# A two-layer block on one core: the step-size chain is moved mostly to GpSimd, C's rows are moved by DMA, and all four engines get a new order in the state-space stage

## What is computed

```python
zxbcdt = u @ W_in.T                    # z 512, x 512, B 64, C 64, dt 4
xBC = silu(conv4(xBC))                 # causal, 4 taps per channel
dt  = softplus(dt + dt_bias)           # per token and head: the step size
A   = -exp(A_log) * dt                 # per token and head: the decay rate
# chunks of 128 tokens:
Y_diag = ((C @ B.T) * exp(segsum(A))) @ (x * dt)
states = decayed previous state + (B * decay).T @ (x * dt)
Y_off  = (C @ previous state) * exp(cumsum(A))
y = (Y_diag + Y_off + D * x) * silu(z); y = rmsnorm(y) @ W_out.T
x3 = layernorm(x2 + y)
```

## Time and profile before

| | us |
|---|---|
| median of 3 runs | 1286.04 (1283.23 to 1286.77) |
| profiled execution, its time | 1287.44 |
| profiled execution, its span | 1285.2 |
| PE busy | 1212.8 |
| state-space steps | from 652 to 989 |

### The profile page before, as it was taken

How to read it: one execution, slowest core, us unless ns; L and a number is a source line. 1 busy time by engine, 2 the same in 40 slices (tenths; PEclk the granted TensorE clock), 3 DMA queues, 4 the chain that set the end, 5 groups by cost and what they waited for, 6 DMA issues and landing times.

```text
span 1285.2 us, 20958 instructions
## 1 busy us (share of the span) xinstructions
PE 1212.8 (94%) x7192; PEld 1033.5 (80%) x7192; DVE 853.5 (66%) x1590; ACT 612.3 (48%) x1240; POOL 444.8 (35%) x577
## 2 busy tenths in 40 slices
PE   6899999999999999999989999999998899999994
PEld 5777888888888888888867777777776788888884
DVE  4787635444353535443668988889853889999995
ACT  3443323232333323233467878888874444444441
POOL 0345200000000000000068878878773334444343
PEclk8999999999999999999989999999998899999998
DMA  5222101001010101000000101111010101111100
GB/s 181 83 82 86 34 1 30 5 1 34 1 34 1 33 0 43 6 1 17 13 30 25 39 10 45 45 45 37 8 46 25 34 1 33 33 33 33 33 17 33
DMA packets 30393, 41.29 MB, mean 32 GB/s; under 512 B 2432, under 2 KB 22912, under 8 KB 30208
## 3 DMA queue, kind: packets, MB, share of 16 engines
q1 hardware_dynamic: 30336, 40.53, 9.7%
HBM read 27.94 MB, written 12.58 MB: 32 GB/s over the span
## 4 chain that ended last, share of the span: by engine, by line
PE 75%; DVE 15%; issue 4%; ACT 3%; POOL 2%; DMA 1%; DVEq 0%; POOLq 0%; ACTq 0%; SPq 0%; PEldq 0%
PE bank L45 23%; PE bank L47 22%; PE bank L46 22%; DVE acc L1260 3%; PE bank L1854 1%; DVE mag L1090 1%; PE bank L1835 1%; DVE acc L1256 1%; ACT hh L719 1%; PE bank L1759 1%; DVE dden L1281 1%; DVE wf L1098 1%; PE bank L1594 1%; PE bank L1816 1%; DVE hb L1166 1%
## 5 line engine op out<-in xcount | busy, mean ns | idle before, releaser
L1166 DVE TENSOR_TENSOR hb<-gl,bank 128x512 f32<-128x512 f32 x128 | 87.9, 687 | 198.9 <-PE bank L47 196.3
L719 ACT ACTIVATE hh<-hb 128x512 fp32r<-128x512 f32 x128 | 80.9, 632 | 182.9 <-DVE hb L1166 182.9
L758 ACT ACTIVATE gl<-bank 128x512 f32<-128x512 f32 x128 | 76.4, 597 | 180.7 <-PE bank L47 180.5
L1129 DVE TENSOR_TENSOR hl<-hb,hh 128x512 fp32r<-128x512 f32 x128 | 96.3, 752 | 84.5 <-ACT hh L719 84.5
L702 POOL TENSOR_TENSOR dhl<-dab,dhh 128x512 fp32r<-128x512 f32 x64 | 96.5, 1529 | 141.8 <-ACT dhh L719 141.8
L547 POOL TENSOR_TENSOR veb<-mvb,eps 128x4 f32<-128x4 f32 x8 | 1.8, 228 | 377.7 <-DVE mvb L1146 377.7
L45 PE MATMUL bank<-xt_l,w_h 128*128 128x512 f32 x256 | 105.4, 412 | 8.8 <-DVE xt_l L1129 4.5
L47 PE MATMUL bank<-xt_h,w_h 128*128 128x512 f32 x256 | 103.2, 403 | 0.0
L45 PE MATMUL bank<-at_l,w_hi_a 128*128 128x512 f32 x256 | 102.5, 400 | 0.5 <-PE bank L47 0.3
L46 PE MATMUL bank<-xt_h,w_l 128*128 128x512 f32 x256 | 103.0, 402 | 0.0
L47 PE MATMUL bank<-at_h,w_hi_a 128*128 128x512 f32 x256 | 101.7, 397 | 0.0
(11 more groups left out here) (234 smaller groups left out, 3642.7 us busy)
## 6 DMA issues: line engine op xcount, KB each, us to landing
xg<-x_scratch SPq DMA_DIRECT2D x16, 512.0 KB, 4.0
xall<-in_x SPq DMA_DIRECT2D x8, 512.0 KB, 7.6
xg<-in_xt SPq DMA_DIRECT2D x8, 512.0 KB, 5.0
x_scratch<-rows_out SPq DMA_DIRECT2D x8, 512.0 KB, 3.2
x_scratch<-rows_out SPq DMA_DIRECT2D x16, 256.0 KB, 2.2
out<-rows_out SPq DMA_DIRECT2D x8, 512.0 KB, 3.1
wq<-in_codes SPq DMA_DIRECT2D x12, 256.0 KB, 2.7
sc<-in_scales SPq DMA_DIRECT2D x12, 256.0 KB, 2.9
```

What stands on the lines that cost most here:

```text
L719: return act.activation(dst, src, ACT.Copy)
L758: act.activation(gl[:, n % 2], ps_gate[n % 2][:], ACT.Gelu_apprx_tanh).then_inc(s_gelu, 1)
L1129: return dve.tensor_tensor(dst, src, hi.bitcast(F32), ALU.subtract)
L1166: dve.tensor_tensor(hb[:, n % 2], gl[:, n % 2], ps_up[n % 2][:], ALU.mult).then_inc(s_h, 1)
```

## The change

- `dt_ratio` and `dt_and_rate` go from DVE to POOL. DVE keeps four instructions: the bias, -|d|, u, and one reciprocal (`dt_inverse`). The guard on u - 1 and the one on the logarithm are replaced by one maximum in the instruction that makes u. POOL gets seven small `tensor_tensor` for a group, max(d, 0) made as a subtraction and a multiplication. One more in all negates the decay rate ahead of the first.
- `c_rows` (C's 64 partitions copied to partitions 0 to 63, `ct`) goes from a DVE copy to a DMA on SP's queue, except for the first group.
- `inv_std_chunk` for each chunk becomes `inv_std_pair` for two chunks.
- The lanes of PSUM are dealt anew, and with them the waits; all four `step` functions have another order. SP loads the weight piece after the rows instead of ahead of them, since `mlp1_low` stands later on POOL.

```diff
-DT_STEPS = 11
+DT_STEPS = 4
+DTP_STEPS = 7
+TINY = 2.0 ** -23
...
-        T_LANE = (lane_q, lane_p)
-        DT_LANE = lane_p
-        XBC_LANE = (lane_q, lane_r, lane_q, lane_r, lane_r)
-        def acs_lane(n):
-            return lane_q if isinstance(n, int) and n == 0 else lane_p
+        T_LANE = (lane_p, lane_q)
+        XBC_LANE = (lane_p, lane_r, lane_p, lane_r, lane_q)
+        ACS_LANE = lane_q
+        def dt_lane(n):
+            return lane_p if isinstance(n, int) and n == 0 else lane_r
         def z_lane(n, t):
             if isinstance(n, int) and n == 0:
                 return (lane_p, lane_r, lane_r, lane_p)[t]
-            return (lane_p, lane_p, lane_p, lane_q)[t]
+            return (lane_q, lane_q, lane_p, lane_q)[t]
         def seg_lane(t, more=True):
-            return (lane_r, lane_p, lane_r if more else lane_q, lane_p if more else lane_q)[t]
+            return (lane_r, lane_r, lane_r, lane_p)[t] if more or t == 0 else lane_q
...
+            def c_rows(n, b):
+                sp.wait_ge(c_silu, XB * n + 1)
+                sp.dma_start(ct[:, b], bc[D_STATE:2 * D_STATE, b]).then_inc(c_ct, 16)
...
             def step(s, b, i, more):
                 k = NT * s
                 if more or b == 0:
-                    sp.wait_ge(c_w1l, s + 1)
-                    sp.dma_start(w1_raw[:], w_mlp1[s + 1]).then_inc(c_w1r, 16)
+                    c_rows(s + 1, 1 - b)
                 if more:
                     sp.wait_ge(c_rest, s + 1)
                     sp.dma_start(xg[:, b], x2_rows[b * GPB + i + 1]).then_inc(c_xg[b], 16)
@@ -485,6 +494,9 @@
                         sp.wait_ge(c_x3st[half], 16 * s + 16)
                     sp.wait_ge(c_rest, s + 1)
                     sp.dma_start(xg[:, 0], x3_rows[0]).then_inc(d_x, 16)
+                if more or b == 0:
+                    sp.wait_ge(c_w1l, s + 1)
+                    sp.dma_start(w1_raw[:], w_mlp1[s + 1]).then_inc(c_w1r, 16)
                 store_x3(b, i, 0, k)
...
+            def dt_ratio(n):
+                pool.wait_ge(c_dtc, DT_STEPS * n + 3)
+                pool.tensor_tensor(um[:], du[:], ones[:, 0:NT * HEADS], ALU.subtract).then_inc(c_dtq, 1)
+                pool.tensor_tensor(dtwo[:], dax[:], d_flat, ALU.subtract).then_inc(c_dtq, 1)
+                pool.wait_ge(c_dtq, DTP_STEPS * n + 2)
+                pool.tensor_tensor(dpos[:], dtwo[:], m_half[:, 0:1].broadcast_to([P, NT * HEADS]), ALU.mult).then_inc(c_dtq, 1)
+            def dt_and_rate(n, b):
+                pool.wait_ge(c_dtc, DT_STEPS * (n + 1))
+                pool.tensor_tensor(dq[:], de[:], drec[:], ALU.mult).then_inc(c_dtq, 1)
+                pool.wait_ge(c_dta, 2 * n + 2)
+                pool.wait_ge(c_dtq, DTP_STEPS * n + 4)
+                pool.tensor_tensor(dm2[:], dq[:], dl[:], ALU.mult).then_inc(c_dtq, 1)
+                pool.wait_ge(c_dtq, DTP_STEPS * n + 5)
+                pool.tensor_tensor(dtv[:, b].rearrange("p t h -> p (t h)"), dpos[:], dm2[:], ALU.add).then_inc(c_dtq, 1)
+                pool.wait_ge(c_dtq, DTP_STEPS * n + 6)
+                if not isinstance(n, int) or n > 0:
+                    pool.wait_ge(c_acs, n)
+                pool.tensor_tensor(adt[:], dtv[:, b], na4[:].unsqueeze(1).broadcast_to([P, NT, HEADS]),
+                                   ALU.mult).then_inc(c_dtq, 1)
             def rates_split(n):
-                pool.wait_ge(c_dtc, DT_STEPS * (n + 1))
+                pool.wait_ge(c_dtq, DTP_STEPS * (n + 1))
...
+            def inv_std_pair(k, c):
+                two = slice(c, c + 2)
+                pool.wait_ge(c_ln3, 2 * k + 4)
+                pool.tensor_tensor(ve[:, two], mv[:, two, 1], eps4[:, 0:2], ALU.add).then_inc(c_ln3r, 1)
+                pool.wait_ge(c_ln3r, 2 * k + 1)
+                pool.tensor_tensor(rstd[:, two], ve[:, two], m_half[:, 0:2], ALU.pow).then_inc(c_ln3r, 1)
+                pool.tensor_tensor(nmr[:, two], wide_i[:, 0:2], mv[:, two, 0], ALU.subtract).then_inc(c_ln3r, 1)
+                pool.wait_ge(c_ln3r, 2 * k + 3)
+                pool.tensor_tensor(nmr[:, two], nmr[:, two], rstd[:, two], ALU.mult).then_inc(c_ln3r, 1)
...
+                if nxt:
+                    halo_terms(n, nxt[1])
+                x_skip(k + 1, 1)
                 gate_rows(k, 0, 0)
-                mlp1_low(s)
-                x_skip(k + 1, 1)
+                if before:
+                    inv_std_pair(k - 2, 2)
+                y_off_skip(k + 1, 1)
                 inv_rms(k, 0)
-                if before:
-                    inv_std_chunk(k - 2, 2)
-                y_off_skip(k + 1, 1)
-                if before:
-                    inv_std_chunk(k - 1, 3)
+                x_skip(k + 2, 0)
+                if nxt:
+                    dt_ratio(n)
+                y_off_skip(k + 2, 0)
                 gate_rows(k + 1, 1, 1)
-                x_skip(k + 2, 0)
-                y_off_skip(k + 2, 0)
-                if nxt:
+                if nxt:
+                    dt_and_rate(n, nxt[1])
                     rates_split(n)
                     masked_decay(n, 0)
                 gate_rows(k + 2, 0, 2)
                 x_skip(k + 3, 1)
+                inv_rms(k + 1, 1)
                 y_off_skip(k + 3, 1)
-                inv_rms(k + 1, 1)
-                inv_std_chunk(k, 0)
+                if nxt:
+                    masked_decay(n, 1)
...
             def dt_one_plus(n):
                 dve.wait_ge(c_dta, 2 * n + 1)
-                dt_done(n, 3, dve.tensor_scalar(du[:], de[:], 1.0, None, ALU.add))
-            def dt_ratio(n):
-                dt_done(n, 4, dve.tensor_scalar(um[:], du[:], -1.0, None, ALU.add))
-                dt_done(n, 5, dve.scalar_tensor_tensor(dden[:], um[:], 0.0, um[:], ALU.is_equal, ALU.add))
-                dt_done(n, 6, dve.reciprocal(drec[:], dden[:]))
-                dt_done(n, 7, dve.tensor_tensor(dm1[:], de[:], drec[:], ALU.mult))
-            def dt_and_rate(n, b):
-                dve.wait_ge(c_dta, 2 * n + 2)
-                dt_done(n, 8, dve.scalar_tensor_tensor(dl2[:], um[:], 0.0, dl[:], ALU.is_equal, ALU.add))
-                dt_done(n, 9, dve.tensor_tensor(dm2[:], dm1[:], dl2[:], ALU.mult))
-                dt_done(n, 10, dve.scalar_tensor_tensor(dtv[:, b].rearrange("p t h -> p (t h)"), d_flat, 0.0, dm2[:],
-                                                        ALU.max, ALU.add))
-                if not isinstance(n, int) or n > 0:
-                    dve.wait_ge(c_acs, n)
-                dt_done(n, 11, dve.scalar_tensor_tensor(adt[:], dtv[:, b], -1.0, a4[:].unsqueeze(1).broadcast_to([P, NT, HEADS]),
-                                                        ALU.mult, ALU.mult))
+                dve.tensor_scalar(du[:], de[:], 1.0, 1.0 + TINY, ALU.add, ALU.max).then_inc(c_dtc, 1)
+            def dt_inverse(n):
+                dve.wait_ge(c_dtq, DTP_STEPS * n + 1)
+                dve.reciprocal(drec[:], um[:]).then_inc(c_dtc, 1)
...
+                    dt_one_plus(n)
+                b_weighted(k + 3, 3, 1)
                 g_lo(k, 0)
-                cb_mask(k + 2)
-                y_sum(k + 1, 1)
-                new_state(s, b, k + 1, 1)
-                if nxt:
-                    dt_ratio(n)
-                mixing(k + 2, 2, 0)
-                if nxt:
-                    dt_and_rate(n, nb)
+                if nxt:
+                    conv(n, nb, 0)
+                    dt_inverse(n)
+                new_state(s, b, k + 2, 2)
+                y_sum(k + 2, 0)
                 add_out(s, b, k, 0, 0)
                 if nxt:
                     conv(n, nb, 1)
                 else:
                     gated1(0, 0, 1, bank[1])
-                y_sum(k + 2, 0)
-                new_state(s, b, k + 2, 2)
-                cb_mask(k + 3)
-                rows_stats(k, 0)
                 mixing(k + 3, 3, 1)
                 g_lo(k + 1, 1)
                 if nxt:
                     conv(n, nb, 2)
+                add_out(s, b, k + 1, 1, 1)
                 y_sum(k + 3, 1)
-                add_out(s, b, k + 1, 1, 1)
-                b_weighted(k + 3, 3, 1)
                 if nxt:
                     conv(n, nb, 3)
                 else:
                     gated1(0, 0, 2, bank[1])
                 g_lo(k + 2, 0)
-                if nxt:
-                    c_rows(n, nb)
...
+                scores_cb(k + 3, b, 3)
+                y_diag(k + 1, 1)
+                g_transpose(k, 0)
+                x_token_major(k + 2, b, 2)
+                state_add(k + 1, 1)
                 if nxt:
                     in_proj_at(n, 0)
-                g_transpose(k, 0)
-                y_off(k + 1, b, 1)
-                scores_cb(k + 2, b, 2)
-                segment_sums(s, 3, nxt is not None)
-                y_diag(k + 1, 1)
-                x_token_major(k + 2, b, 2)
+                y_off(k + 2, b, 2)
                 if nxt:
                     in_proj_at(n, 1)
                 else:
                     mlp1_first(1)
```

(80 more changed lines are left out.)

179 lines of the change are left out of this document (91 added, 88 removed).

## The result

| | before | after |
|---|---|---|
| median, us | 1285.15 (4 runs, 1283.23 to 1286.77) | 1261.47 (4 runs, 1260.87 to 1262.96) |
| ratio | | 0.9818, 95% interval 0.980 to 0.9836 |
| span of the profiled execution | 1285.2 | 1261.0 |
| a middle step | 40.78 | 38.46 |

The kernel is 1.8% faster; forecast were 1267.5 and 1260 to 1278. The stretches of the new trace (us, busy PE, PEld, DVE, ACT, POOL, clock, DMA share, GB/s) answer to the earlier trace rows: a middle step, the last step up to the end of its last `out_proj`, the first step, and the piece of it at the lower clock.

What follows compares the result with a forecast made beforehand. PE was taken to bound the state-space stage. Middle steps -13.2, first -2, last -4, lead-in +0.4 and tail +0.3 sum to -18.5: 1268.9 against 1287.4 profiled, 1267.5 at the median, range 1260 to 1278.

Steps and rivals of the forecast that it cites:

- 38.1 of work and 0.4 of new waits: Middle step: PE's work 38.5 less 0.4 for fewer three-pass runs, plus 0.4 of new conv waits; 2.2 below 40.7.
- rival D: More gain: no new wait and runs at full value, 37.75 us a step, last step -7, 1260 us; chance 0.13.
- The two waits of the earlier trace: PE's waits once a middle step each for add_out and a conv, worth 1.38 and about 0.8, together 2.2 us.
- The margins: Time to spare before PE would wait at four places in a middle step's new order: 0.5 to 0.7 us each.
- by itself nothing on the path: DVE's relief, about 4 us a step from the chain and 1.01 from C's rows, gains nothing directly.
- rival A: Half a gain: POOL and DVE block each other, new waits 1.5 us a step instead of 0.4, 1276 us; chance 0.20.
- Chain onto POOL: Seven small dependent POOL instructions at 0.26 us apiece, about 1.8 us a step; the skill's factor two would at most double it.
- "-2" for the first: First step of the state-space stage: same waits removed, but partly at the lower clock, so 2 us gained.
- "-4" for the last: Last step of the stage: fewer waits for PE in the new order, 4 us gained, between 0 and 8.
- Lead-in and tail: First masked decay later by 0.4 us (0 to 1.2); last two norms as one pair cost 0.3 at the end.
- B: No change: the two waits return at segment_sums(n, 0) and out_proj(k + 2), 2.2 us a step, 1283 to 1288; chance 0.06.
- C: Slower: POOL's um waits for a late du on DVE, holding up add_out(k) and PE; 1289 us; chance 0.06.

Runs made afterwards that it cites:

- e12: The kernel before, in its old order, with only the step-size chain moved to POOL: 1271.78 us, ratio 0.9884 to the kernel before.
- e3: The changed kernel's new order with chain, C's rows and norms all undone: 1269.95 us, ratio 0.9869 to the kernel before.
- e11: The changed kernel with C's rows copied on DVE again, norm pairs kept: 1260.71 us, ratio 0.9801 to the kernel before.
- e2: The changed kernel with C's rows copied on DVE and norms single again: 1259.98 us, ratio 0.9797 to the kernel before.
- e1: The changed kernel with the step-size chain back on DVE: 1270.84 us, ratio 0.9879 to the kernel before.
- e5: The changed kernel itself, measured again beside the other runs: 1262.61 us, ratio 0.9813 to the kernel before.
- e8: The changed kernel with the state's memset behind the first masked decay and a gate-and-up pair behind the last g_transpose: 1261.04 us, ratio 0.981 to the kernel before.
- e4: The kernel before, in its old order, with chain on POOL, C's rows by DMA and norms in pairs: 1275.79 us, ratio 0.9922.

## Why the prediction was right, and where it was off

**Middle steps: right in size, off in the split.** 38.5 was forecast as 38.1 of work and 0.4 of new waits; measured are 38.46 and 0. That the sum came out is luck: two errors of 0.4 cancel. Against the 38.5 that I read out of the old trace, the work fell by 0.04, not 0.4. The base was read too low: e12, in the old order, has PE busy for 38.73 of 39.13 us, so the new order saves 0.2 to 0.3 of work (rival D had 0.75). The two waits of the earlier trace rows were worth 2.1 (predicted 2.2). The margins were close: `g_transpose(k + 1)` 0.51 (0.5); `segment_sums(n, 0)` 0.83 (0.7); `out_proj(k + 2)` 0.22 behind `g_lo` (0.5); `in_proj_at(n, 3)` 0.06 (0.6). From the end of `out_proj(k)` DVE needed the predicted 3.3 and one hit of 0.8, 4.1 in all; PE's blocks took 4.15 instead of 3.9. At 3.9 PE would have waited 0.2: the missing wait and the missing saving of work are partly the same thing.

**What the gain came from.** Neither the order nor the chain is the cause alone: -1.2 us a step for the order (e3), -1.65 for the chain alone (e12), -2.3 for both, which overlap in the same two waits. C's rows by DMA bring nothing in the new order (e11, e2), nor can a gain of the pairs be seen; the forecast had only the chain's and C's relief of DVE down as "by itself nothing on the path", and that holds for C's.

**Port blocking (rival A).** It happens: `du` took 0.86 and the conv's head 0.95, both ending with a POOL instruction. The Trainium skill's rule ("SBUF — State Buffer", Who interferes with whom) describes this, and the trace agrees. But the hit on the conv fell into a margin, and the one on `du` did not reach PE, since DVE stood idle for 0.60 us ahead of `add_out(k)`. Rival A's mechanism was there, its price was not.

**Chain onto POOL.** Predicted 0.26 between dependent steps, measured 0.31 (789.68 - 789.37); DVE's steps in e1 took 0.17 against 0.23. The 0.19 that I gave for 16 columns was a misreading: the earlier trace rows has it for one column, and 16 take 0.22 to 0.23. The Trainium skill's factor of two ("GPSIMD Engine Reference", Engine selection) does not show at 16 columns. At 512 it nearly does: 1.28 for POOL's `gate_rows`, 0.68 for DVE's `y_sum`. DVE's 31.25 (30.5 to 31) and POOL's 32.23 (32.6, even) came as said. So did C's rows: 806.63 - 800.4 = 6.2 us to spare (6).

**First and last step: the waits right, the clock missed.** These two terms hold 5.1 of the 5.7 us between -18.5 and -24.2. The steps of the prediction that were off are "-2" for the first and "-4" for the last: I took the clock of before as given. Three stretches of before: the first step's piece at the lower clock, the last step, and all that is behind it; then what is behind the last step after.

```profile
649.20:659.40 10.20, 9.77 (x43) 7.60 (x41) 2.80 (x6) 4.95 (x15) 7.76 (x13) 0.50 0.16 53
940.19:988.83 48.64, 40.25 (x245) 32.12 (x245) 21.37 (x50) 26.31 (x67) 27.44 (x48) 0.91 0.05 17
988.83:1285.20 296.37, 273.41 (x1546) 237.73 (x1545) 250.93 (x413) 125.89 (x211) 114.45 (x84) 0.97 0.09 28
```

```profile
964.00:1261.00 297.00, 275.17 (x1546) 239.00 (x1544) 250.25 (x413) 126.59 (x212) 114.54 (x84) 0.96 0.09 28
```

The lower level (1.2 GHz) lasted 10.2 us at the first step before, and 3.3 after. PE's busy time in that step fell by 2.8 us (40.73 to 37.94), where a middle step's fell by 0.5: some 2.3 of the -4.4 is clock, by this estimate. In the last step the clock rose from 0.91 to 0.99; PE's idle time there fell from 8.4 to 5.05 us (I had counted 4.4 of waits to be left), and its busy time by 3.3 as well. But more than half of this clock was not won, it moved: behind the last step the clock fell from 0.97 to 0.96, and the same number of matmuls kept PE busy for 1.8 us more. That leaves about 1.5 us of clock in the last step and behind it, and about 4 in the whole gain of 24.2. The mean granted clocks of the two profiled executions, 0.981 and 0.985, stand for 48.8 and 37.8 us at the lower level, which allows at most 5.5. Nor does the order alone set the clock: in 35 executions of the kernel before, its mean went from 0.980 (1287.77 us) to 0.986 (1283.84 us). 649.20 to 661.80 in e1, e12, e2 and e5, in this order:

```profile
649.20:661.80 12.60, 11.92 (x59) 9.37 (x58) 5.20 (x13) 7.23 (x20) 9.85 (x15) 0.59 0.13 43
```

```profile
649.20:661.80 12.60, 11.40 (x47) 9.08 (x48) 3.83 (x8) 6.14 (x17) 9.88 (x15) 0.59 0.01 2
```

```profile
649.20:661.80 12.60, 11.58 (x62) 9.12 (x63) 5.21 (x13) 7.38 (x21) 11.16 (x16) 0.73 0.01 3
```

```profile
649.20:661.80 12.60, 10.74 (x64) 8.51 (x65) 5.78 (x14) 7.82 (x22) 11.50 (x17) 0.86 0.00 1
```

All seven kernels with the chain on DVE or in the old order have 0.59 or 0.60 in this stretch, about 10 us at the lower level; of those with both changes e2 has 0.73 (6.8 us), the others 0.86 (3.3 to 3.5). That is one trace of each. PE's longest wait just ahead is 2.9 to 3.2 us in all of them, so that is not the difference. What is, stays open. The lower level costs time only where nothing else holds PE: in e2 it lasted twice as long as in e5, and the first step was still shorter (38.63, 39.22), since PE then stood only 0.2 instead of 1.3 us for the memset behind it.

**Lead-in and tail.** 3.25 us instead of 2.91 for the first masked decay (+0.3; predicted +0.4). I missed that the state's memset, behind four decays that begin later, then comes 0.9 later to PE (1.29 instead of 0.43); e8 shows that it can go. Behind the last step +0.6 (+0.3).

**The rivals.** B and C did not come in this kernel; a wait like C's is what e4 shows, where the chain's first half is placed worse. D has the time (1260), but by another sum: it wanted 37.75 us a step, which nothing came near. Its "no new wait" held, and its -7 for the last step was met (-6.7), but half of it was clock, most of which was lost again behind the step. D's 1260 is also set against the profiled time; at the median it would be 1258.6.

## What to carry to other kernels

Where two engines wait for each other in a ring, moving work off the late one and moving the waiting instruction behind other work overlap; measure each alone before adding them, and then ask what the next queue (here SP's, behind a store) makes late. A copy handed to a DMA queue is free only if nothing ahead of it in that queue is released late. Count the clock's lower level as something that can change with a new order, and from one execution to the next, with its own range; and look behind the stretch that became faster before calling clock time won.
